# Cross attention: where the turn of a pair's normalised rows and its output projection stand in TensorE's order

## The reference

```python
x = x + attention(layernorm(x), W_qkv)                  # causal, one head
x = x + cross(layernorm(x), ctx, mask, Wq..Wo, bq..bo)  # 16 heads of 8
x = x + ffn(layernorm(x), w_gate, w_up, w_down)         # levels of 16 and 4 bits
```

```python
scores = q @ k.T / sqrt(8)                       # 128 x 128
scores = where(mask == 0, -1e9, scores)
out    = softmax(scores) @ v                     # 128 x 8
x      = concat_heads(out) @ Wo.T + bo           # 128 x 128
```

## Time and profile before

| | before |
|---|---|
| median of 3 runs | 334.16 us |
| the profiled execution | 334.31 us, of which the trace spans 332.5 us |
| granted TensorE clock in the cross stage | 1.00 of full speed |
| busy, whole span: TensorE, VectorE, ScalarE, GpSimd | 91%, 83%, 78%, 58% |
| chain that ended last: TensorE, VectorE, ScalarE, GpSimd | 58%, 17%, 8%, 7% |
| VectorE maxima, L1594, x128 | 84.8 us, 686 ns each |
| ScalarE exponentials, L1258, x64 | 76.8 us, 1201 ns each |

### The profile page before, as it was taken

How to read it: one execution, slowest core, us unless ns; L and a number is a source line. 1 busy time by engine, 2 the same in 40 slices (tenths; PEclk the granted TensorE clock), 3 DMA queues, 4 the chain that set the end, 5 groups by cost and what they waited for, 6 DMA issues and landing times.

```text
span 332.5 us, 9933 instructions
## 1 busy us (share of the span) xinstructions
PE 303.8 (91%) x3741; PEld 205.8 (62%) x3741; DVE 276.1 (83%) x652; ACT 258.5 (78%) x470; POOL 192.2 (58%) x339
## 2 busy tenths in 40 slices
PE   2899999999999999999999999999986689697996
PEld 1587877877656666666666665854432244357996
DVE  5359999868879999999999994777789996889754
ACT  3267988887889989999898998788797768993940
POOL 3467999894238698768657678300067773781000
PEclk9999999999999999999999999999999999999999
DMA  5891335662101556500000000000000000000134
GB/s 154 257 288 34 96 120 185 193 201 95 48 23 64 156 170 191 162 4 5 3 2 5 4 3 4 0 1 0 2 0 0 1 1 2 0 0 1 34 95 128
DMA packets 23754, 22.70 MB, mean 68 GB/s; under 512 B 3545, under 2 KB 21402, under 8 KB 23578
## 3 DMA queue, kind: packets, MB, share of 16 engines
q1 hardware_dynamic: 22170, 21.78, 21.3%
q10 hardware_dynamic: 1536, 0.28, 0.5%
HBM read 15.75 MB, written 6.31 MB: 66 GB/s over the span
## 4 chain that ended last, share of the span: by engine, by line
PE 58%; DVE 17%; ACT 8%; POOL 7%; issue 6%; DMA 2%; SPq 1%; POOLq 0%; ACTq 0%; DVEq 0%
PE banks L707 9%; PE banks L763 9%; PE banks L989 8%; DVE mxs L1820 7%; PE banks L1059 7%; PE banks L637 4%; DVE nm L1594 3%; PE banks L785 3%; PE banks L630 3%; ACT ng L1355 2%; PE banks L781 2%; POOL rstd L380 2%; PE banks L776 2%; PE banks L649 2%; PE banks L971 2%
## 5 line engine op out<-in xcount | busy, mean ns | idle before, releaser
L1594 DVE TENSOR_REDUCE nm<-banks 128x4 f32<-128x512 f32 x128 | 84.8, 686 | 6.2 <-PE banks L707 2.6
L1258 ACT ACTIVATE PT<-banks,bmask,vmask 128x1024 f32<-128x1024 f32 x64 | 76.8, 1201 | 2.7
L989 PE MATMUL banks<-X3T,upT 128*128 128x512 f32 x96 | 44.3, 601 | 11.5 <-DVE mxs L1820 8.9
L576 POOL TENSOR_TENSOR G<-ng,sq 128x1536 int32<-128x1536 int32 (+3 forms) x10 | 27.9, 2796 | 36.4 <-DVE sq L1851 36.4
L707 PE MATMUL banks<-kd,qd 32*128 32x128 f16 x512 | 47.6, 217 | 0.7 <-DVE nm L1594 0.4
L1820 DVE TENSOR_REDUCE mxs<-G 128x1 f32<-128x1536 int32 (+3 forms) x30 | 42.2, 1424 | 4.3 <-ACT G L1316 3.8
L763 PE MATMUL banks<-PT,VP 128*32 128x128 f32 x1024 | 41.2, 279 | 0.0
L707 PEld LDWEIGHTS banks<-kd,qd 32*128 32x128 f16 x512 | 27.0, 92 | 20.6 <-issue 11.8
L989 PEld LDWEIGHTS banks<-X3T,upT 128*128 128x128 f32 x96 | 17.4, 191 | 34.2 <-issue 15.8
L1100 ACT ACTIVATE h<-X,shift,rstd 128x128 f32<-128x128 f32 x64 | 26.3, 483 | 10.2 <-POOL shift L425 10.2
L763 PEld LDWEIGHTS banks<-PT,VP 128*32 128x32 f32 x1024 | 24.1, 109 | 9.3 <-issue 3.2
(11 more groups left out here) (200 smaller groups left out, 735.2 us busy)
## 6 DMA issues: line engine op xcount, KB each, us to landing
kd<-k_dram SPq DMA_DIRECT2D x32, 128.0 KB, 2.7
qd<-q_dram SPq DMA_DIRECT2D x32, 128.0 KB, 2.7
ctxg<-in_ctx_dram SPq DMA_DIRECT2D x8, 256.0 KB, 3.1
X3T<-m_dram SPq DMA_DIRECT2D x1, 1792.0 KB, 10.0
out_dram<-y SPq DMA_DIRECT2D x7, 256.0 KB, 2.3
X<-in_x_dram SPq DMA_DIRECT2D x3, 512.0 KB, 9.7
k_dram<-khi SPq DMA_DIRECT2D x7, 128.0 KB, 1.9
k_dram<-klo SPq DMA_DIRECT2D x7, 128.0 KB, 1.9
```

The lines of the kernel that those rows point to most:

```text
L576: nc.gpsimd.tensor_tensor(GI[:, c], ng[:, u, part], sq[:, u, part], ALU.mult).then_inc(S["b_t"], 1)
L989: m = pe.matmul(bank(2 + FC * (g % 2) + k), w[:, k * P:k * P + P], grp(X3T, g), start=True, stop=True)
L1258: act.activation(PT[:, a, :], bank(2 + 2 * a, 2), ACT.Exp, bias=bmask[:, n:n + 1], scale=vmask[:, n:n + 1]).then_inc(S["t_exp"], 1)
L1594: V.tensor_reduce(nm[:, n % 2, c:c + NSET], bank(u).rearrange("p (h m) -> p h m", m=P), AX.X, ALU.max, negate=True).then_inc(S["t_max"], 1)
```

## The change

In each pair the turn of the normalised rows is issued behind both half-banks of a = 0 in place of between them, and the projection behind both half-banks of a = 1 in place of between them. No instruction is added or removed; the lists of the other engines are the same.

```diff
                 first_half_bank(n, 0)
+                second_half_bank(n, 0)
                 if n > 0:
                     turn(n - 1)
-                second_half_bank(n, 0)
                 if n == 0:
                     queries2(NG - 1)
                 pe.wait_ge(S["t_exp"], 2 * n + 2)
                 pv(n, 1)
                 first_half_bank(n, 1)
-                if 0 < n and n != B - 2:
-                    project(n - 1)
                 second_half_bank(n, 1)
-                if n == B - 2:
+                if n > 0:
                     project(n - 1)
```

## The result

The changed kernel takes 335.04 us (median of 14 runs, 334.44 to 335.71), the kernel before 334.2 us (median of 14 runs, 333.08 to 334.72) beside it. The ratio is 1.0026 with a 95% interval of 1.0016 to 1.0036: slower by 0.26%, just beyond what can be told from no change. The forecast of 334.3 was 0.7 us too low. The time lies in the range of 8 in 10, but outside the range of the likeliest case (333.7 to 334.9): it is the slower case, which had a chance of 0.25.

What follows compares the result with a forecast made beforehand. TensorE's list and an equally long circle through ScalarE, 3.58 us a pair, were taken as the bound. Ordinary pairs 0 and late pairs +0.2 us on the 334.16 median gave 334.3 us; 8-in-10 range 333.2 to 336.3.

Steps and rivals of the forecast that it cites:

- likeliest case: Whole kernel: no measurable change, 334.3 us with its own range from 333.7 to 334.9; chance 0.57.
- The bound: In ordinary pairs TensorE's list and a circle through ScalarE are equally long, within 0.02 us, at 3.58 us.
- the share would fall below 96%: Sign of being right: TensorE, newly idle ahead of L776, has a busy share below 96% in the stretch.
- The second rival: TensorE's list counts and ScalarE's circle gives way; pairs fall towards VectorE's busy 3.39 us: 329.7 us; chance 0.06.
- TensorE's list: Joined half-banks save 0.14 us at the first place, 0.17 at the second: 3.27 us a pair, turned into idle time.
- The circle through ScalarE: Products, scores, injections, turn, its copy, exponential, output copy, next products: 3.58 to 3.59 us after, 3.58 before.
- the six waits: Every fourth pair, the turn idles for VectorE's `on_`, making the pair 0.13 us longer; all six go, 0.8 us.
- The hidden path: Ordinary pairs: maxima, injections, projection, its copy, next products take 3.52 us, hidden with a slack of 0.06 us.
- ordinary pairs stay at 3.58: Sign of being right: pairs without the late VectorE work keep their length of 3.58 us; change 0 +-0.4 us.
- The late pairs: Pairs behind VectorE's four aggregations: products wait for the projection's copy, 3.75 to 3.79 us in five; net +0.2 us.
- The faster rival of the late pairs: Pairs behind the four aggregations lose their 0.13 us wait and nothing replaces it: 333.4 us; chance 0.12.
- The slower rival: Hand-over from output copy to transposes (L776) costs 0.07 us more in 27 pairs: +1.9 us, 336.2 us; chance 0.25.

Runs made afterwards that it cites:

- run with the largest moved: Changed kernel with VectorE's largest of the rows (0.32 us) moved from ahead of the first two maxima to behind them: 334.53 us, ratio to before 1.0001.
- copy behind the exponential: Changed kernel with ScalarE's copy of the turn moved from ahead of the next exponential to behind it: 335.69 us, ratio to before 1.0039.
- four such runs: Projection's copy `wo` or turn's copy `oT` made 0.10 us longer: 337.48 and 335.93 us on the changed kernel, 332.41 and 336.08 with the turn alone moved.
- projection alone: Kernel before with only the projection moved behind both half-banks, the turn left between the half-banks: 335.6 us, ratio 1.0037.
- longer `wo`: Changed kernel with ScalarE's copy of the projection 256 columns wide in place of 128, 0.10 us longer: 337.48 us.
- half copy: Kernel with the turn alone moved, ScalarE's output copy cut in two halves, the first ahead of the turn's copy: 333.98 us, ratio to before 0.9987.

## Why the prediction was right or wrong

**The bound.** Right in kind. TensorE's busy share in the stretch is 98% in the changed kernel, with a list that is shorter, and the pair is longer. The Trainium skill, page "Perfetto Trace Analysis", section "Identifying the Most-Contended Engine", would have looked for a gain at the busiest engine, with the reservation that TensorE's matmul busy share is not a good measure of how close it is to roofline (the prediction's word "flatters" gives this a direction that the page does not). The runs agree with the reservation: the share is 98%, yet the starts leave some 0.36 us of a 3.63 us pair unused (an estimate: the list of 3.27 worked out in the prediction). For the same reason the sign that the share would fall below 96% failed to appear. The second rival, 329.7 us by a VectorE bound, did not come.

**TensorE's list.** Scores to injections 0.24 against 0.23 to 0.24; turn to products 0.26 as taken; projection to `max_rows` 0.32 in the range of 0.26 to 0.43. The saving is real and unused, as said. At the second place scores and injections lie 0.39 apart and not the 0.23 that was named as a sign: there the injections wait for the maxima.

**The circle through ScalarE.** Forecast 3.58 to 3.59. Alone in force, with only the turn moved, it measures 3.57, and its terms are the forecast ones within 0.02. That the copy of the turn holds up the exponential was right (0.38 idle ahead of `oT` in every pair), and that this costs an ordinary pair nothing was right as well: by itself the move of the turn gains 2.0 us. The prediction had the six waits that go with the turn and the late pairs that come with the projection, but only as one sum of +0.2. The gain of the turn (in its trace 1.20 in the 27 pairs, mostly the six waits of 0.13, and 0.2 ahead of pair 3) would have shown, had I worked out each move alone.

**The hidden path.** This is the step that failed: "In ordinary pairs ... the same path gives 1.00 + 1.28 + 0.05 + 0.33 + 0.53 + 0.28 + 0.05 = 3.52. It is hidden, by only 0.06 us." It is 3.63 and on top, by 0.06. Of the 0.11 missing, 0.09 is the last term: from the end of the projection's copy to the products it takes 0.14 (0.11 to the weight load), and I had taken 0.05 from another pair of instructions, `on_` to the turn. The rest is roundings. 22 pairs at 3.63 in place of 3.58 are 1.0 us (0.044 each before rounding). The sign "ordinary pairs stay at 3.58" failed with it.

**The late pairs.** Forecast 3.75 to 3.79, measured 3.79 to 3.80, in the five pairs named, with the sixth like the ordinary ones; the run with the largest moved shows the cause. Here two errors cancel, which is luck: the last term is 0.09 longer here as well, so that from the reciprocal to the next products it takes 3.42 and not 3.33, and the reciprocal comes 0.38 behind the products (144.84 and 144.46), not 0.42 to 0.46.

**The faster rival of the late pairs** (333.4, nothing takes the place of their wait) did not come either: it holds for the turn alone, where they fall to 3.57, and not with the projection moved.

**The slower rival** gave 336.2 us at +0.07 a pair for a longer hand-over at L776. Size and sign came near (+0.05 a pair), the mechanism was another: at L776 the step from the copy costs 0.05 to 0.06, no more than the 0.05 taken (for the 0.12 of pair 30 see the last section), and a run in which TensorE does not wait there at all (the copy behind the exponential) is no shorter. That the hidden path "would work in the same direction" stood only in a remark at its end; it was the cause. That the measured time fell into the range owes more to this rival's price, set for another reason, than to the sum: the range was right in part by luck.

## What to carry to other kernels

Where engines hand work round in a loop, write down every closed path from an instruction to its next instance and sum it, also those that seem hidden; a path with a slack below the uncertainty of its terms is a case of its own and not a footnote. Work out each move of a change alone before both together: here one gains 2.0 us, and the other, on top of it, loses 2.6. To learn which of two waits that end at nearly the same time is the bound, lengthen each by a known amount and see whether the loop takes it over in full: four such runs separated 0.06 us.

The best version found is the turn alone moved: 332.42 us, 0.51% below the kernel before and 0.8% below the changed one.

## What the runs showed of the hardware

A step from the end of a ScalarE copy to the weight load that waits for it was 0.05 to 0.06 us at L776 (151.40 to 151.46) and 0.11 at L763 (151.75 to 151.86), with 0.11 again in other kernels (projection alone, copy behind the exponential, largest behind, longer `wo`, half copy). At L776 the copy delivers what is loaded, and at L763 it frees a PSUM bank; but at pair 30 of the kernel before L776 took 0.12 as well, so the use of the copy does not explain the difference.

What goes with it in every trace is where the wait stands. The first line is of the kernel before, the second of the changed one; `PEldq` is the sequencer ahead of TensorE's weight loads, and the durations are in ns:

```profile
L774 PEldq EVENT_SEMAPHORE  x1: 51/51/51, 205.4 to 205.4; - x1
L929 PEldq EVENT_SEMAPHORE  x29: 51/51/51, 100.6 to 202.9; - x29
```

L929 is the wait for `t_wc`, the projection's copy, ahead of the products. Two waits stand in front of them, `t_vp` and `t_wc`; the load carries the first, and the second is an instruction of its own, which lasts 0.05. In the changed kernel it runs from 151.79 to 151.84, 0.04 behind the end of the copy and 0.02 ahead of the load. At L776 the load carries the wait for the output copy itself, in all pairs but one: behind pair 30 there is no `max_rows`, two waits stand in a row, and the one for the copy is L774, a separate instruction (205.39 to 205.44), just where the step is 0.12. Over the eleven traces, where TensorE stood waiting for a ScalarE copy, the step to L776 is 0.050 to 0.052 in 164 cases with the wait carried by the load, and 0.113 to 0.115 in the 9 with it in a separate instruction; to L763 it is 0.112 to 0.114 in 147 cases, all separate. So of the 0.09 by which the last term of the hidden path was too small, about 0.06 is this second instruction. No run changed the order of the two waits. By an estimate from these figures, with the wait for `t_wc` carried by the load, the changed kernel's path of 3.63 would be 3.57, as long as the circle through the exponential.

A chain that ends behind such a wait showed its idle time as ended by "issue" in most pairs, not by the copy: the bound of the changed kernel appears in only five pairs under the name of `wo`, the late ones.
